# Token rows of the expert tiles in four column pieces, turned by VectorE, with the gate on the down product

## The reference, cut to what matters

```python
probs = softmax(x @ w_router); topk_vals, topk_idx = top_k(probs, 2)
up = x @ w_up[e]; gate = silu(x @ w_gate[e])
exp_out = (up * gate) @ w_down[e]          # 128 -> 512 -> 128
out = 2.0 * topk_vals[..., 0:1] * exp_out  # only where topk_idx[..., 0] == e
return x + out + (x @ ws_up * silu(x @ ws_gate)) @ ws_down
```

## Time and profile before

| | us |
|---|---|
| median of three runs | 359.43 (357.93 to 362.31) |
| span of the profiled execution | 365.6 |
| TensorE busy | 330.0 (90%) |
| VectorE busy | 225.6 (62%) |
| ScalarE busy | 176.4 (48%) |
| GpSimd busy | 174.9 (48%) |
| granted TensorE clock, mean | 0.973 of full |

### The profile page before, as it was taken

The page is one execution under the profiler, slowest core; times in us unless marked ns, Lnnn a source line. Parts: engine busy times, 40 slices in busy tenths (PEclk is TensorE's granted clock), DMA queues, the critical chain, the costliest instruction groups (busy, mean ns, idle before and its releaser), DMA issues. The chain is left out here.

```text
span 365.6 us, 12604 instructions
## 1 busy us (share of the span) xinstructions
PE 330.0 (90%) x5014; PEld 260.7 (71%) x5014; DVE 225.6 (62%) x539; ACT 176.4 (48%) x313; POOL 174.9 (48%) x256
## 2 busy tenths in 40 slices
PE   8788999899999898997967999979999999999980
PEld 8545665565656555885855888868898999989970
DVE  4966997788988978779442333333555455554540
ACT  1646666567666575663221222214455554555530
POOL 6652455464557566692674444462333333333331
PEclk9989999999999999999889999998999999999996
DMA  8965333334433321000121111213222232222200
GB/s 207 357 219 149 90 109 98 97 105 129 133 101 100 102 44 32 2 2 0 37 86 56 67 61 60 88 43 81 77 66 65 69 73 71 67 67 69 74 5 0
DMA packets 40426, 30.66 MB, mean 84 GB/s; under 512 B 5792, under 2 KB 36772, under 8 KB 40370
## 3 DMA queue, kind: packets, MB, share of 16 engines
q1 hardware_dynamic: 36800, 23.17, 23.0%
q0 software_dynamic: 2880, 6.43, 5.0%
q10 hardware_dynamic: 690, 0.26, 0.4%
HBM read 13.72 MB, written 11.95 MB: 70 GB/s over the span
## 5 line engine op out<-in xcount | busy, mean ns | idle before, releaser
L599 POOL DMA_INDIRECT out<-y,tok_u x38 | 37.4, 984 | 72.8 <-DVE y L1199 72.8
L1214 DVE SCALAR_TENSOR_TENSOR Pr<-psS,xs,PT 128x256 f32<-128x256 f32 x76 | 33.3, 480 | 47.6 <-PE psS L1549 47.3
L881 DVE TENSOR_REDUCE row_max<-psS 128x16 fp32r<-128x1024 f32 x32 | 39.1, 1224 | 16.3 <-PE psS L1274 16.1
L1025 DVE TENSOR_TENSOR hT<-psS,PT 128x512 f32<-128x512 f32 x32 | 22.1, 690 | 41.4 <-PE psO L1436 17.1
L768 ACT ACTIVATE PT<-psS 128x512 f32<-128x512 f32 x32 | 19.2, 599 | 58.0 <-PE psS L1424 44.6
L1565 PEld LDWEIGHTS psB<-down_sb,Pr 128*128 128x128 f32 x304 | 40.2, 193 | 4.3 <-issue 1.0
L917 DVE STREAM_TRANSPOSE PT<-Pr 128x1024 f32<-128x1024 f32 x32 | 39.6, 1236 | 2.4 <-ACT Pr L671 2.2
L1565 PE MATMUL psB<-down_sb,Pr 128*128 x304 | 40.3, 276 | 0.8 <-ACT Pr L805 0.8
L428 POOL TENSOR_TENSOR rows<-rows,proj 128x128 f32<-128x128 f32 x31 | 14.2, 458 | 54.9 <-ACT proj L677 52.3
L1303 PEld LDWEIGHTS psO<-VD,PT 128*32 128x32 f32 x2048 | 22.3, 109 | 21.7 <-issue 21.1
L1274 PE MATMUL psS<-Kx,Qx 64*32 64x256 f32 x1024 | 35.1, 384 | 0.8 <-issue 0.8
(11 more groups left out here) (202 smaller groups left out, 730.8 us busy)
## 6 DMA issues: line engine op xcount, KB each, us to landing
sorted_rows<-pad_row SPq DMA_DIRECT2D x19, 264.0 KB
VD<-V SPq DMA_DIRECT2D x120, 36.0 KB, 2.4
xs<-sorted_rows SPq DMA_DIRECT2D x38, 66.0 KB, 2.0
base<-sorted_rows SPq DMA_DIRECT2D x38, 64.0 KB, 1.8
rows<-in_L_attn_x SPq DMA_DIRECT2D x8, 256.0 KB, 5.8
gate_sb<-in_L_ffn_w_gate SPq DMA_DIRECT2D x1, 1792.0 KB, 10.3
up_sb<-in_L_ffn_w_up SPq DMA_DIRECT2D x1, 1792.0 KB, 14.7
down_sb<-in_L_ffn_w_down SPq DMA_DIRECT2D x7, 256.0 KB, 3.4
```

The costliest lines, as they stand in the source:

```text
L599: pool.indirect_dma_start(out=out_list, out_offset=bass.IndirectOffsetOnAxis(tok_u[:, r : r + 1], 0), in_=y[:, r, :], in_offset=None, boun ...
L881: nc.vector.tensor_reduce(row_max[:, k % 2, :], s, AX.X, ALU.max).then_inc(max_done, 1)
L1214: nc.vector.scalar_tensor_tensor(out=hs[:, r % 2, h], in0=psS[:, r % 2, h], scalar=xs[:, q, GATE : GATE + 1], in1=sg[:, r % 2, h], op0=ALU ...
```

## The change

**Loads.** The first half of a row in DRAM now holds only the 128 numbers of the token and zeros behind them; gate and token number stand in the second half, behind the base. `load` is four transfers for one tile: piece `a` takes columns 32a to 32a+31 of all 128 rows, and puts them on the 32 partitions from 32a on, four runs of 32 numbers each. `load_base` takes 132 columns instead of 128, waits also for the write of the tile four before (`written`), since GpSimd now reads the token numbers in `base` itself. A `load` now waits for the turn of the tile whose slot it takes (`xT_ready`), and is issued three tiles ahead of `load_base`.

**Turning.** VectorE's transpose turns each 32x32 block in place; with the rows laid out in pieces as above the result `xT` is the whole turned tile (`expert_x`). It is in SBUF. ScalarE and VectorE make high and low part from it. TensorE's turn is gone.

**Gate.** The hidden values are up times silu; the gate multiplies the down product in the instruction that adds the base. The cast of the token numbers is gone: they are written as integers.

**Order on TensorE.** The first of the three gate products stands ahead of the turns of the hidden values (`expert_gate_first`), the other two behind them.

```diff
             def load(i, r, wait=True):
                 if wait:
-                    sp.wait_ge(eh_done, i - (RING - 1))
-                sp.dma_start(xs[:, r, :], sorted_rows[bass.ds(i * P, P), 0:ROW]).then_inc(xs_in[r], 16)
+                    sp.wait_ge(xT_ready, i - (RING - 1))
+                for a in range(NJ):
+                    w = slice(a * BLK, (a + 1) * BLK)
+                    sp.dma_start(
+                        xs[w, r, :, :], sorted_rows[i * P : (i + 1) * P, w].rearrange("(b p) d -> p b d", p=BLK)
+                    ).then_inc(xs_in[r], 16)
             def load_base(i, r, wait=True):
                 if wait:
                     sp.wait_ge(y_ready, i - (RING - 1))
-                sp.dma_start(base[:, r, :], sorted_rows[bass.ds(i * P, P), ROW : ROW + D]).then_inc(base_in[r], 16)
+                    sp.wait_ge(written[r], 16 * (i // RING))
+                sp.dma_start(base[:, r, :], sorted_rows[i * P : (i + 1) * P, ROW:]).then_inc(base_in[r], 16)
...
+            for i in range(RING, 2 * RING - 1):
+                load(i, i % RING)
             for i in range(RING, MT):
-                load(i, i % RING)
+                if i + RING - 1 < MT:
+                    load(i + RING - 1, (i + RING - 1) % RING)
                 load_base(i, i % RING)
...
             def turned_rows(i, r):
-                act.wait_ge(xsT_done, i + 1)
-                nc.scalar.copy(xsT[:, r % 2, 0, :], psA[:, 0:P]).then_inc(xsT_ready, 1)
+                act.wait_ge(xT_ready, i + 1)
+                if r >= 2:
+                    act.wait_ge(eu_done, i - 1)
+                nc.scalar.copy(xsT[:, r % 2, 0, :], xT[:, r % 2, :]).then_inc(xsT_ready, 1)
...
+            def expert_x(i, r):
+                dve.wait_ge(xs_in[r % RING], NJ * loads(i, r))
+                nc.vector.transpose(
+                    xT[:, r % 2, :], xs[:, r % RING, :, :].rearrange("p b d -> p (b d)")
+                ).then_inc(xT_ready, 1)
...
-                    nc.vector.tensor_tensor(y[:, q, :], psB[:, 0:D], base[:, q, :], ALU.add).then_inc(y_ready, 1)
+                    if r - 2 >= RING:
+                        dve.wait_ge(written[q], loads(s - 2, r - 2) - 16)
+                    nc.vector.scalar_tensor_tensor(
+                        out=y[:, q, :], in0=psB[:, 0:D], scalar=base[:, q, GATE : GATE + 1], in1=base[:, q, 0:D],
+                        op0=ALU.mult, op1=ALU.add,
+                    ).then_inc(y_ready, 1)
...
-                    nc.vector.tensor_copy(tok_u[:, q : q + 1], xs[:, q, TOKEN : TOKEN + 1])
...
-                        nc.vector.scalar_tensor_tensor(
-                            out=hs[:, r % 2, h], in0=psS[:, r % 2, h], scalar=xs[:, q, GATE : GATE + 1],
-                            in1=sg[:, r % 2, h], op0=ALU.mult, op1=ALU.mult,
+                        nc.vector.tensor_tensor(
+                            hs[:, r % 2, h], psS[:, r % 2, h], sg[:, r % 2, h], ALU.mult
                         ).then_inc(done, 1)
+                if ug and s + 2 < MT:
+                    expert_x(s + 2, r + 2)
...
-                if xt:
-                    expert_turn_rows(s + 1, r + 1)
                 if fetch:
                     [at[r + 1]] = weights_of(s + 1)
+                if ug:
+                    expert_gate_first(s, r, at[r])
                 if ht:
...
                 if ug:
-                    expert_gate(s, r, at[r])
+                    expert_gate_rest(s, r, at[r])
                     expert_up(s, r, at[r])
```

More of the change, by code:

```diff
@@ L56, in windowed_attention_top1_moe_kernel @@
     RING = 4
-    NOBODY = 2.0 * NT * P
+    NOBODY = 2 * NT * P
     ALPHA, EPS = 2.0, 1e-5
@@ L115, in windowed_attention_top1_moe_kernel @@
         last_mv = sb("last_mv", [P, TPB, 2])
-        xn = sb("xn", [P, TPB, D])
+        xn_base = sb("xn_base", [P, RING * ROW])
+        xn = xn_base[:, 0 : TPB * D].rearrange("p (k d) -> p k d", d=D)
+        base = xn_base[:, :].rearrange("p (r d) -> p r d", d=ROW)
         xnT = sb("xnT", [P, T])
@@ L168, in windowed_attention_top1_moe_kernel @@
         xn2T_lo = sb_over("Kx", "xn2T_lo", [P, NT * P], f32r)
-        xs = sb("xs", [P, RING, ROW])
-        base = sb_over("xn", "base", [P, RING, D])
+        xs = sb("xs", [P, RING, NJ, BLK])
         logitsT = sb_over("xnT", "logitsT", [P, T])
-        first_lo = sb_over("xn", "first_lo", [P, T], f32r)
-        tok_u = sb("tok_u", [P, RING], u32)
-        xsT = sb_over("V", "xsT", [P, 2, 2, P], f32r)
+        first_lo = sb_over("xn_base", "first_lo", [P, T], f32r)
+        tok_u = base[:, :, TOKEN : TOKEN + 1].bitcast(u32)
+        xT = sb_over("V", "xT", [P, 2, P])
+        xsT = nc.alloc_sbuf_tensor_at("xsT", [P, 2, 2, P], f32r, offset=place["V"] + 4 * 2 * P)
         hs = Pr[:, 0, :].rearrange("p (a h) -> p a h", a=2)
@@ L396, in _ @@
             make(pool.memset(power[:, :], -0.5))
-            make(pool.memset(pad_row[:, :, 0:TOKEN], 0.0))
-            pool.memset(pad_row[:, :, TOKEN:], NOBODY).then_inc(pad_ready, 1)
+            make(pool.memset(pad_row[:, :, :], 0.0))
+            pool.memset(pad_row[:, :, ROW + TOKEN :].bitcast(i32), NOBODY).then_inc(pad_ready, 1)
             made_up_to = dict(channel_multiplier=0, allow_small_or_imprecise_dtypes=True)
@@ L401, in _ @@
             make(pool.iota(tile_row[:, :], [[P, MT]], base=0, **made_up_to))
-            make(pool.memset(rows[:, :, 0, TOKEN + 1 :], 0.0))
-            make(pool.memset(rows[:, :, 1, D:], 0.0))
+            make(pool.memset(rows[:, :, 0, D:], 0.0))
+            make(pool.memset(rows[:, :, 1, TOKEN + 1 :], 0.0))
             pool.iota(
-                rows[:, :, 0, TOKEN : TOKEN + 1], [[P, NT], [0, 1]], base=0, channel_multiplier=1,
-                allow_small_or_imprecise_dtypes=True,
+                rows[:, :, 1, TOKEN : TOKEN + 1].bitcast(i32), [[P, NT], [0, 1]], base=0, channel_multiplier=1,
             ).then_inc(consts_ready, 1)
@@ L1076, in gates @@
                 then(nc.vector.reciprocal(esum[:, :], esum[:, :]))
-                nc.vector.tensor_tensor(rows[:, :, 0, GATE], esum[:, :], has_expert[:, :], ALU.mult).then_inc(gates_ready, 1)
+                nc.vector.tensor_tensor(rows[:, :, 1, GATE], esum[:, :], has_expert[:, :], ALU.mult).then_inc(gates_ready, 1)
             flat = "p e g -> p (e g)"
@@ L1184, in _ @@
                 shared_hidden(B - 1, c)
+            expert_x(0, 0)
             expert_low_parts(0, 0)
+            expert_x(1, 1)
             shared_hidden(B - 1, NC - 1)
@@ L1522, in _ @@
             down_flat = down_sb[:, :, :].rearrange("p e h -> p (e h)")
[L1524 to L1528, removed]
             def weights_of(i):
@@ L1535, in weights_of, with expert_gate_first @@
                 return list(starts)
-            def expert_product(s, r, start, half, hi, lo, done):
-                w = bass.ds(start, HID)
-                x_hi, x_lo = xsT[:, r % 2, 0, :], xsT[:, r % 2, 1, :]
+            def expert_gate_first(s, r, start):
                 pe.wait_ge(xsT_lo_ready, s + 1)
@@ L1545, in expert_product, with expert_gate_rest, expert_step @@
                     pe.wait_ge(h_done, B * NC - 1 + r)
[L1546 to L1552, removed]
-            def expert_up(s, r, start):
-                expert_product(s, r, start, 0, up_hi, up_lo, eu_done)
-            def expert_step(s, r, at, ug=True, ht=True, xt=True, down=True, fetch=True):
+                w = bass.ds(start, HID)
+                mm(psS[:, r % 2, 512:], xsT[:, r % 2, 1, :], gate_hi[:, w], start=True, stop=False)
+            def expert_gate_rest(s, r, start):
+                w, x_hi = bass.ds(start, HID), xsT[:, r % 2, 0, :]
+                mm(psS[:, r % 2, 512:], x_hi, gate_lo[:, w], start=False, stop=False)
+                mm(psS[:, r % 2, 512:], x_hi, gate_hi[:, w], start=False, stop=True).then_inc(eg_done, 1)
+            def expert_up(s, r, start):
+                w, x_hi, x_lo = bass.ds(start, HID), xsT[:, r % 2, 0, :], xsT[:, r % 2, 1, :]
+                mm(psS[:, r % 2, 0:512], x_lo, up_hi[:, w], start=True, stop=False)
+                mm(psS[:, r % 2, 0:512], x_hi, up_lo[:, w], start=False, stop=False)
+                mm(psS[:, r % 2, 0:512], x_hi, up_hi[:, w], start=False, stop=True).then_inc(eu_done, 1)
+            def expert_step(s, r, at, ug=True, ht=True, down=True, fetch=True):
                 if down:
@@ L1603, in _ @@
             expert_up(0, 0, at[0])
-            expert_step(0, 0, at, ug=False, ht=False, down=False)
+            [at[1]] = weights_of(1)
             for s in range(1, MT - 1):
                 expert_step(s, s, at, down=s >= 2)
-            expert_step(MT - 1, MT - 1, at, xt=False, fetch=False)
-            expert_step(MT, MT, at, ug=False, xt=False, fetch=False)
-            expert_step(MT + 1, MT + 1, at, ug=False, ht=False, xt=False, fetch=False)
+            expert_step(MT - 1, MT - 1, at, fetch=False)
+            expert_step(MT, MT, at, ug=False, fetch=False)
```

(1 more changed line is left out.)

14 lines of the change are left out of this document (5 added, 9 removed).

## The result

Forecast was 355.8 us with a range to 367.5; measured was a median of **366.6 us** against 358.7 before, a ratio of 1.021 (95% interval 1.012 to 1.030). Later, on a chip where the kernel before takes 369.4, it was 375.5, a ratio of 1.015 (1.008 to 1.023). The median lay inside the range, but by luck: the range went up to 367.5 above all for the rival on SyncE, which didn't come true. The direction was wrong: 4 us faster was forecast, 6 to 8 us slower was measured.

A forecast was written before the change was run, and what follows sets the result against it. TensorE was taken to bound the expert steps at 2.83 us without a gap. The terms -4.2 + 0.6 - 0.6 + 0.6 = -3.6 took 359.43 to 355.8 us; own range 353.8 to 357.5, 8 in 10 from 353.6 to 367.5.

The forecast's parts named there:

- the rival on SyncE: Expert loads: at 0.64 us per piece SyncE becomes the bound, 3.03 us per round, +6 to +11 us; chance 0.25.
- The bound before: Expert steps of the old kernel: TensorE busy 40.00 of 40 us, without a gap, 2.83 us per step.
- TensorE's work: Expert steps: the token rows' turn goes, 38 x 0.11 = 4.2 us saved, no passage cost, new step 2.72 us.
- the moved product at no cost: Expert steps: the first gate product ahead of the four turns adds 0 us; delays on VectorE and ScalarE stay hidden.
- the second rival: The moved product closes a chain through TensorE's sequencer: up to 3.06 us per step, mostly 0 to +3 us; chance 0.12.
- 1.46 + x: Step length of the sequencer chain, copy's end to copy's end; hidden below x = 1.26, 3.06 us at x = 1.60.
- The sign that the prediction itself named: Expert steps, sign of being wrong: a gap before the first gate product with ScalarE and VectorE both done.
- Small packets: Rival: 128-byte runs bind the transfer engines from 69 ns per packet; at 75 ns about +3 us; chance 0.06.
- VectorE: Expert steps: transpose 0.31, output 0.3, hidden values 0.88 us; busy 1.8 of 2.72, so nothing shows.
- The beginnings: Start of the expert stage: +0.6 at tile 1's transpose, -0.6 at the passage, +0.6 at tile 4's late rows.
- The first part: Tile 1's transpose stands ahead of the shared expert's last hidden values, which start at 239.2 instead of 238.62: +0.6 us.
- The 2.61 of waiting in the earlier trace: VectorE's adds at 244.63 come late for an unshown reason and may stay; passage gain taken as -0.6, between 0 and -1.5.

The follow-up runs named there:

- double_read: The changed kernel with TensorE's read of the weight position done twice in a row: steps of 3.63 us, 393.8 us in one run.
- before_gate_first: The kernel before with only the first gate product moved ahead of the turns of the hidden values: steps of 3.10 us, median 380.1 us, ratio 1.031.
- before_read_at_end: The kernel before with the read of the weight position moved behind the up product: steps of 2.86 us, median 367.7 us, ratio 0.996.
- read_at_end: The changed kernel with the read of the weight position moved behind the up product: steps of 2.73 us, median 365.6 us, ratio 0.984.

## Why the prediction was wrong, step by step

- **The bound before** was read rightly: TensorE without a gap, 2.83 us per step.
- **TensorE's work** was sized rightly: 0.11 per turn, no price for the passage between number formats, 2.72 in sum; 2.72 to 2.73 measured as soon as the read is out of the chain or the product back in its place. Over the 35 steps that is 4.4 us against the kernel before, 3.9 by the prediction.
- **The step that failed** is the moved product at no cost: "one of them only moves ahead of the four turns", "Nothing of this shows, I say", and the chance of 0.12, "mostly at 0 to +3", for the second rival. The mechanism was in the text with the right formula, 1.46 + x, where x is the time from the copy's end to the moved product. But x was taken as unknown below 1.60, "and most values below leave it hidden or at some tenths". Measured, x is 1.48 in the mean of 27 steps, well over the point of 1.26 from which it shows. 0.60 of it is the read, by double_read; of the other 0.88, 0.38 go by before the down product's first record, and what the sequencer does in the rest no run separates. The formula gives 2.94 for it; the rest up to 3.03 is that the product took 0.33 instead of 0.23. Its weight load starts just when the gap ends and not behind the down product, which would explain it, but no run separates that. So the step took 3.03 and not 2.72: 9.9 us over the stretch (104.9 against 95.0), which wipes out the 4.4 and adds 5.5. The sign that the prediction itself named came true, a gap before the first gate product with ScalarE and VectorE both done.
- **SyncE, first rival** (0.25): wrong. A piece took 0.432 in the median and four with a gap 1.87, so 0.47 each, as forecast; SyncE waited 15 times in about 27 rounds. So the number of partitions was not what made `VD<-V` dearer; the source, SBUF there and DRAM here, is what is left, and no run separates it from the shape.
- **Small packets** (0.06): wrong too. The queue's row from 260 to 340 us answers to the earlier trace rows:

```profile
q1 hardware_dynamic: 19759, 3.69, 28.9%
```

  16 x 80 us x 28.9% over 19759 packets is 19 ns each, less than the 33 before and far from the 69 at which they would bind. By the byte they are dearer: nearly the same data (3.69 MB, 3.73 before) took 28.9% of the engines' time and not 20.7%, 1.4 times as much. The Trainium skill (DMA: Bandwidth & Descriptors, Specifications) has 512 B as the least for full rate, and that agrees; the read-modify-write that it gives as the reason can't be seen in the trace, and the 75 ns of the prediction didn't come of it.
- **VectorE**: transposes 0.30 (0.31), output 0.34 (0.3), hidden values 0.76 (0.88 taken), and no wait for rows in the steady steps. Right.
- **The beginnings**: net +0.6 forecast. The first part, VectorE's last shared hidden values behind a transpose, was +0.6: they come 1.50 us behind the ones before them in the kernel before, 1.83 in the second profile of the change, and 3.31 in the first, where the transpose waited 1.51 for its rows. From the last but one of these to the output of tile 2 it takes 19.5 us before and 19.9 and 19.2 in the change; but before_gate_first, with the same loads as before, takes 19.2, and before_read_at_end 18.4. The clock may be a part of that: in the profile before, TensorE was granted 0.59 of it from 246 to 250 us, in the two others 1.00. The 2.61 of waiting in the earlier trace rows is no part of it, for these two have it as well (2.57 and 2.58). So +0.6 is not refuted, and single profiles differ by more than that; what each wait costs stays open.

## What to carry to other kernels

A busy engine can be bound by its own instruction stream: add up, for each step, the chain from one engine's result through the waiting instruction, all that is issued behind it in order (register reads above all) and back, and compare it with the busy sum. It costs nothing until it is longer. Before an instruction moves into such a chain, measure how much slack it has, for instance by doubling one piece of it; and put register reads where the sequencer would wait anyway.

## What the runs showed of the hardware

- One read of an SBUF value to a TensorE register, with the two register instructions behind it, lengthened the chain through the instruction stream by 0.60 us (3.63 against 3.03 per step). Issued behind the moved product, beside the array's work, it cost 0.04 (2.77 against 2.73). The Trainium skill gives about 600 ns as the floor of a `tensor_load` (DMA: Bandwidth & Descriptors, Latency and other measured facts); the trace agrees.
- A 512-column product behind a gap took 0.34 us from its start to the next (301.06 to 301.40 in the change), one without a gap 0.23 to 0.24 (the later products of the step; the moved one in read_at_end).
- Loads from DRAM to 32 partitions in runs of 128 bytes took 0.43 us to issue and 1.9 to land, copies from SBUF to SBUF of 32 partitions 0.60 to issue.
